# Packed weights unpacked in an earlier layer, biases spread out, two products and one load moved: a fused eight-layer kernel on one core

## What is computed

```python
# layer 1: attention, 16 heads of 96 (second_attention); then the rotated feed-forward
x = x + attention_1(norm(x), ctx)
x = x + (hadamard(norm(x)) @ W.T + b + lora(norm(x)))
# layer 2: attention, 32 heads of 128, queries and keys RMS-normed (wide_attention)
q, k = rmsnorm(norm(x) @ Wq.T), rmsnorm(ctx @ Wk.T)
x = x + softmax(q @ k.T / sqrt(128) + mask) @ v @ Wo.T
x = x + dequant(fp8(norm(x)) @ fp8(weight))         # quantised_ffn
# layer 3: autocorrelation attention (lag_attention); then a feed-forward on packed weights
x = x + lag_attention(norm(x), ctx)
w = interleave(words >> 4, words << 28 >> 28) * scale_of_each_64     # w1, w2, w3
x = x + (silu(norm(x) @ w1.T) * (norm(x) @ w3.T)) @ w2.T
```

## Time and profile before

| | us |
|---|---|
| median of 3 runs (1535.88 to 1538.91) | 1538.39 |
| the profiled execution, its own time | 1534.98 |
| the profiled execution, span of the instructions | 1533.3 |
| second_attention | 353.7 to 651.3 |
| rotated_ffn | 652.3 to 683.8 |
| wide_attention | 684.4 to 1206.1 |
| quantised_ffn | 1207.1 to 1247.5 |
| lag_attention | 1248.4 to 1352.9 |
| packed feed-forward | 1353.8 to 1533.3 |

### The profile page before, as it was taken

One profiled execution on the slowest core, in us unless ns is written; L12 is line 12 of the kernel. 1 busy time (PEld: TensorE's weight loads), 2 busy tenths in 40 slices (PEclk: granted clock), 3 DMA queues, 4 the chain that ended last, 5 costly groups with the idle time before them and its releaser, 6 DMA issues. The chain is left out here.

```text
span 1533.3 us, 31435 instructions
## 1 busy us (share of the span) xinstructions
PE 1386.9 (90%) x11352; PEld 829.4 (54%) x11352; DVE 1063.9 (69%) x2135; ACT 757.5 (49%) x2424; POOL 722.3 (47%) x750
## 2 busy tenths in 40 slices
PE   5888699997999999779999999999998777779998
PEld 4676344445777777335555555555554334334444
DVE  7997565635767666568878878788777779955212
ACT  4777363222424433338666666666654456555111
POOL 4887451002443444836666666666556115744000
PEclk9999699999999999989999999999999889989999
DMA  7999572215999988666667666555546302355000
GB/s 187 186 173 175 125 170 42 37 33 137 178 186 188 168 137 143 116 163 134 119 128 114 118 128 119 111 110 107 107 77 135 94 3 49 95 96 111 14 15 28
DMA packets 524137, 174.62 MB, mean 114 GB/s; under 512 B 482528, under 2 KB 507424, under 8 KB 523856
## 3 DMA queue, kind: packets, MB, share of 16 engines
q1 hardware_dynamic: 523984, 172.62, 58.4%
HBM read 53.27 MB, written 2.10 MB: 36 GB/s over the span
## 5 line engine op out<-in xcount | busy, mean ns | idle before, releaser
L1943 POOL TENSOR_TENSOR a_q_ss<-a_q_ss,half 128x4 f32<-128x4 f32 x64 | 90.1, 1408 | 170.0 <-DVE a_k_ss L1853 90.7
L67 PE MATMUL bank<-a_wq_hi,xn_pair 128*128 128x512 f16 (+1 forms) x384 | 139.8, 364 | 14.2 <-issue 8.3
L1767 ACT ACTIVATE a_probs<-a_masked,a_negmax 128x128 f32<-128x128 f32 x256 | 99.6, 390 | 96.9 <-DVE a_negmax L1824 96.9
L1286 POOL TENSOR_TENSOR a_p_hl<-a_probs,a_p_hl 128x512 f16<-128x512 f32 x64 | 74.3, 1161 | 142.4 <-DVE a_p_hl L1210 142.4
L69 PE MATMUL bank<-a_wq_hi,xn_pair 128*128 128x512 f16 (+1 forms) x384 | 139.6, 364 | 0.0
L68 PE MATMUL bank<-a_wq_lo,xn_pair 128*128 128x512 f16 (+1 forms) x384 | 139.6, 364 | 0.0
L67 PE MATMUL bank<-a_wo_hi,a_o_hi 128*128 128x512 f16 x256 | 98.4, 384 | 3.5 <-DVE x_state L1840 3.5
L68 PE MATMUL bank<-a_wo_lo,a_o_hi 128*128 128x512 f16 x256 | 98.0, 383 | 0.0
L69 PE MATMUL bank<-a_wo_hi,a_o_lo 128*128 128x512 f16 x256 | 97.9, 382 | 0.0
L1821 DVE TENSOR_TENSOR a_masked<-bank,a_mask 128x512 f32<-128x512 f32 x64 | 44.1, 690 | 70.5 <-PE bank L69 70.5
L1958 POOL TENSOR_TENSOR a_normal<-a_probs,a_recip 128x512 f32<-128x512 f32 x64 | 89.9, 1404 | 5.0
(11 more groups left out here) (465 smaller groups left out, 4993.9 us busy)
## 6 DMA issues: line engine op xcount, KB each, us to landing
a_no<-in_L_xattn_Wo SPq DMA_DIRECT2D x9, 1024.0 KB, 5.8
a_nq<-in_L_xattn_Wq SPq DMA_DIRECT2D x8, 1024.0 KB, 5.9
a_n_wq<-in_L_xattn_Wq SPq DMA_DIRECT2D x4, 768.0 KB, 6.1
a_n_wo<-in_L_xattn_Wo SPq DMA_DIRECT2D x4, 768.0 KB, 5.8
a_nk<-in_L_xattn_Wk SPq DMA_DIRECT2D x9, 256.0 KB, 3.0
a_nv<-in_L_xattn_Wv SPq DMA_DIRECT2D x9, 256.0 KB, 3.5
f_v_hat<-in_L_ffn_w SPq DMA_DIRECT2D x2, 1152.0 KB, 5.5
x_state<-in_x SPq DMA_DIRECT2D x8, 256.0 KB, 4.8
```

The source lines that it names most:

```text
L67: pe.matmul(out, lh, rh, start=start, stop=False)
L1286: pool.tensor_tensor(p_hl[s % PN][:, 1, t, :], probs[unit(s, t) % PROBS][:, :, :].rearrange("p h n -> p (h n)"), p_hl[s % PN][:, 0, t, :], ...
L1767: m = act.activation(probs[s % 2][:, h, :], src, ACT.Exp, bias=negmax[s % 2][:, h:h + 1], accum_out=total[s % 2][:, h:h + 1])
L1943: pool.tensor_tensor(r[:, :], r[:, :], K.half[:, 0:n], ALU.pow).then_inc(root_done.sem, 1)
```

## The change

1. **Biases.** The seven additions in `second_attention` become five, one row at each of the steps 30 to 34; rows 5 and 6 are added on POOL at the start of `rotated_ffn`, next to row 7.
2. **Turned rows.** The buffers of the normalised rows and their arrival semaphores go to `Rotated`. SP no longer waits at the end of `second_attention`; PE waits for each batch's row in `rotated_ffn`.
3. **Two query products.** `MADE` grows by the query products of the first two batches. They are made at the end of `rotated_ffn` on PE.
4. **Packed words.** A new class `PackedFirst` holds words, scales and the unpacking. SP loads them in wide attention (five transfers at step 0, then w2's words in four parts at steps 2, 4, 6 and 8). One of 13 pieces begins every 4 steps from step 3: DVE shifts at s and s + 2, ACT makes it 16-bit at s + 3, and for w1 and w3 POOL scales at s + 5, ACT splits at s + 6 and DVE at s + 7. All of this leaves `quantised_ffn` and `lag_attention`; what stays there is scaling and splitting of w2's chunks.
5. **First turns.** The two turns of w1 and w3 move from the end of `lag_attention`'s SP program to step 7.
6. **Context.** Its two loads move from step 62 to step 64, behind the turn of the probabilities of unit 63; the weight stays at 62.

```diff
@@ Rotated
+    XB, BIASED = 4, 5
@@ second_attention
-    BIAS_AT = {TOTAL + i: [2 * i - 2, 2 * i - 1] for i in range(1, 4)}
-    BIAS_AT[TOTAL + 4] = [6]
+    BIAS_AT = {ROWS_ROT + 2 + b: [b] for b in range(rot.BIASED)}
...
-                for b in range(rot.AHEAD - XB, rot.AHEAD):
-                    sp.wait_ge(next_in[b % XB], 16 * (b // XB + 1))
@@ wide_attention
+                    down.load(sp, s)
                     if s == LOAD:
...
                         quant.load_weight(sp, weight_in)
+                    if s == TOTAL:
                         quant.load_context(sp, quant_in)
...
+                    down.halves(act, s)
...
+                    down.unpack(dve, s)
...
+                    down.scale_first(pool, s)
@@ WideFirst
-    MADE = (("k", 0, 0), ("k", 0, 1))
+    MADE = (("k", 0, 0), ("k", 0, 1), ("q", 0), ("q", 1))
...
     def make(self, pe, use, bank):
+        if use[0] == "q":
+            b, H = use[1], self.A.heads
+            pe.wait_ge(self.lo_done.sem, self.lo_done.count(("wq", H - 1)))
+            pe.wait_ge(self.next_in[b], 16)
+            for k in range(KT):
+                m = pair_matmul(pe, bank[:, :], tuple(p[:, k, b * P:(b + 1) * P] for p in self.xn),
+                                tuple(p[:, k, 0:H * R] for p in self.w_p["wq"]), k == 0, k == KT - 1)
+            m.then_inc(self.made, 1)
+            return
@@ rotated_ffn
+                    else:
+                        pe.wait_ge(rot.next_in[b % rot.XB], 16 * (b // rot.XB + 1))
...
-                    if b == LAST:
-                        dve.wait_ge(last_biased, 1)
+                    if b in late:
+                        dve.wait_ge(biased.sem, biased.count(b))
...
+                for b in late:
+                    if b == LAST:
+                        pool.wait_ge(last_xn_done, 1)
+                    pool.tensor_tensor(K.x[:, b, :], K.x[:, b, :], rot.bias(), ALU.add).then_inc(biased.sem, 1)
@@ quantised_ffn
-                packed.load_down(sp, words_here)
-                packed.load_first(sp, words_here)
-                sp.wait_ge(words_here, 96)
@@ lag_attention
+                    if i == B - 1:
+                        sp.wait_ge(qb_bank.filled("x"), qb_bank.n_filled("x", B - 1))
+                        for m in ("w1", "w3"):
+                            packed.turn_first(sp, m)
...
-                for m in ("w1", "w3"):
-                    sp.wait_ge(down.lo_done.sem, down.lo_done.count(down.FIRST[m]))
-                    packed.turn_first(sp, m)
...
-                    for chunk in UNPACK.get(i, ()):
-                        down.to_half(act, chunk)
...
-                    for chunk in UNPACK.get(i, ()):
-                        down.unpack(dve, chunk)
...
-                        down.unpack(dve, W3)
...
-                down.scale(pool, W1)
-                down.scale(pool, W3)
-                down.low(pool, W1)
-                down.low(pool, W3)
@@ PackedFirst (new)
+    WORD_PARTS = [(0, 3), (3, 6), (6, 9), (9, 11)]
+    BEGIN = 3
...
+    def piece_at(self, s, late, every):
+        i, odd = divmod(s - self.BEGIN - late, every)
+        return [self.pieces[i]] if odd == 0 and 0 <= i < len(self.pieces) else []
...
+    def unpack(self, dve, s):
+        for part in range(2):
+            for n in self.piece_at(s, 2 * part, 4):
...
+                if part == 0:
...
+                    dve.tensor_scalar(dst[:, 0:g, 0, :], src, 4, None, ALU.arith_shift_right)
+                else:
+                    dve.tensor_scalar(dst[:, 0:g, 1, :], src, 28, 28, ALU.logical_shift_left,
+                                      ALU.arith_shift_right).then_inc(self.ints_done.sem, 1)
```

More of the change, by code:

```diff
@@ L2733, in _, with quantised_ffn @@
                         root(b)
-def quantised_ffn(K, Q, spectra, packed):
+def quantised_ffn(K, Q, spectra):
     nc, LAST = K.nc, B - 1
@@ L2752, in quantised_ffn @@
         row_mean, row_root, const_done = (K.sem(f"f2_{n}") for n in ("row_mean", "row_root", "const"))
-        largest_done, chain, words_here = (K.sem(f"f2_{n}") for n in ("largest", "chain", "words"))
+        largest_done, chain = (K.sem(f"f2_{n}") for n in ("largest", "chain"))
         one, along = sb("one", [1, 2], F32), sb("along", [1, 2, P], F32)
@@ L3222, in step @@
                         r.then_inc(row_mean_done, 1)
-                        down.unpack(dve, W1)
                     if l == B - 1:
@@ new lines, in __init__ @@
+        self.first = {n: m for m, n in self.FIRST.items()}
+        self.chunks = list(range(-(-self.HID * self.PER // self.CHUNK)))
+        self.pieces = list(self.first) + self.chunks
+        step = lambda n, of: Steps(K.sem(f"early_{n}"), of)
+        self.ints_done, self.half_done = step("ints", self.pieces), step("half", self.pieces)
+        self.scaled_done, self.hi_done, self.lo_done = (step(n, list(self.first)) for n in ("scaled", "hi", "lo"))
+        self.first_here, self.scales_here = K.sem("down_first_here"), K.sem("down_scales_here")
@@ new lines, in __init__, with groups, words_of, scales_of @@
+        self.words_here = [K.sem(f"down_words_here{i}") for i in range(len(self.WORD_PARTS))]
+    def groups(self, n):
+        return self.PER if n in self.first else min(self.PER, self.W2G - self.PER * n)
+    def words_of(self, n):
+        if n in self.first:
+            return self.first_words[self.first[n]][:, :]
+        at = self.CHUNK // 2 * n
+        return self.words[:, at:at + self.groups(n) * self.GROUP]
+    def scales_of(self, n):
+        at = 2 * self.PER * n
+        return self.scales[:, at:at + 2 * self.groups(n)]
@@ new lines, in halves @@
+    def halves(self, act, s):
+        for n in self.piece_at(s, 3, 4):
+            i = self.pieces.index(n)
+            act.wait_ge(self.ints_done.sem, self.ints_done.count(n))
+            act.activation(self.values(n), self.ints[i % 2][:, 0:self.groups(n), :, :].rearrange("p j h c -> p (j h c)"),
+                           ACT.Copy, scale=WS).then_inc(self.half_done.sem, 1)
+        for n in self.piece_at(s, 6, 4):
+            if n in self.first:
+                act.wait_ge(self.scaled_done.sem, self.scaled_done.count(n))
+                act.activation(self.first_halves[self.first[n]][:, 0, :], self.flat[self.pieces.index(n)],
+                               ACT.Copy).then_inc(self.hi_done.sem, 1)
@@ new lines, in scale_first @@
+    def scale_first(self, pool, s):
+        for n in self.piece_at(s, 5, 4):
+            if n in self.first:
+                by = self.first_scales[self.first[n]][:, :].unsqueeze(2).to_broadcast([P, 2 * self.PER, self.GROUP])
+                pool.wait_ge(self.half_done.sem, self.half_done.count(n))
+                pool.tensor_tensor(self.flat[self.pieces.index(n)].rearrange("p (j c) -> p j c", c=self.GROUP),
+                                   self.values(n).rearrange("p (j c) -> p j c", c=self.GROUP), by, ALU.mult).then_inc(self.scaled_done.sem, 1)
@@ L3408, in __init__ @@
         self.rows = rows[0:W.PER]
-        step = lambda n: Steps(K.sem(f"down_{n}"), self.pieces)
-        self.ints_done, self.half_done, self.scaled_done, self.hi_done, self.lo_done = (
-            step(n) for n in ("ints", "half", "scaled", "hi", "lo"))
+        step = lambda n: Steps(K.sem(f"down_{n}"), self.chunks)
+        self.scaled_done, self.hi_done, self.lo_done = (step(n) for n in ("scaled", "hi", "lo"))
         self.blank, self.turned = K.sem("down_blank"), W.turned
@@ L3837, in build @@
                 rotated_ffn(K, rot, nxt, first)
+                K.in_use.extend(rot.next_in)
                 K.end_stage()
-            stage_4_to_7(K, a, out, nxt, first, late)
+                K.in_use = kept
+            stage_4_to_7(K, a, out, nxt, first, late, down)
 def stage_0_to_1(K, a, early):
@@ L3853, in stage_2, with stage_4_to_7 @@
     K.in_use.extend(early.first_in.values())
-def stage_4_to_7(K, a, out, nxt, first, late):
+def stage_4_to_7(K, a, out, nxt, first, late, down):
     with ExitStack() as rows:
-        K.xn_rows = rows.enter_context(K.nc.sbuf_tensor("xn_rows", [P, B, DIM], F32))
         quant = Quantised(K, rows, a["L2_ffn_weight"], a["ctx_4096"])
-        wide_attention(K, W2, first, quant, nxt)
+        wide_attention(K, W2, first, quant, nxt, down)
         K.in_use.extend(first.sems())
```

152 lines of the change are left out of this document (67 added, 85 removed).

## The result

The changed kernel takes 1526.39 us (median of 4 runs, 1526.17 to 1527.74); the kernel before, timed beside it, 1538.65 (1535.88 to 1542.34). The ratio is 0.9923, with an interval of 0.9906 to 0.9939: 12.3 us less. The forecast was 1526.7 us, and 11.7 us less. Measured a second time, the changed kernel took 1525.6 against 1538.21, ratio 0.9913 (0.9899 to 0.9926), 12.6 us less.

The account below looks back on a forecast made before the run. PE bounds the middle of wide attention; at the joints, the stage's last engine or first awaited work does. Gains 2.0 - 0.8 + 0 + 3.0 + 3.7 + 3.8 = 11.7 us, from 1538.39 to 1526.7; range 1518 to 1533.

Parts of the forecast that it names:

- Biases and turned rows: End of second_attention: POOL's last additions no longer end the stage; gain 2.0 us, bounds 1.0 and 3.4.
- The delay carried through to the merge: second_attention: early additions delay the last probabilities' low half by 0.87 us; 1.4 us carried to PE's merge and DVE.
- Two query products: End of rotated_ffn grows by 0.8 us (0 to 1.5); wide attention's start gets nothing back, since PE waits there.
- The rival at 1521.5: Start of wide attention: PE was the bound, so 5.2 us of products count; 1521.5 us, chance 0.10.
- Packed words in wide attention: Middle of wide attention: loads and 26 shifts cost 0, hidden behind PE in DVE's 1.6 us idle per step.
- Context later: End of wide attention: unit 62's turn lands earlier, the mix starts 2.5 us earlier; gain 3.0 us, bounds 2.5 and 3.6.
- it escapes the half clock that followed PE's wait: End of wide attention: the mix's first matmul took 0.58 us against 0.38 at full clock; taken as 0.5 us gain.
- my 1190.44: End of wide attention: time when DVE's low half of unit 61 ends, frees the bank and lets the mix start.
- Start of the lag layer: Chunks before the first query product (2.1 us) and search (2.15) go; 3.7 us, between 3.2 and 4.2 by clock rise.
- End of the lag layer: Without the turns of weights SP ends with the rows; the end comes 3.8 us earlier (3.3 to 3.9).
- the two in which the gain is given back: Lag steps, last heads: half given back (1532.5 us, chance 0.09); nearly all given back (about 1537 us, chance 0.07).
- the slower one: Wide attention: shifts break PE's rhythm as DVE and POOL collide; 0.65 us each, 16.9 us, time 1543.6; chance 0.08.

Follow-up runs that it names:

- before: The kernel without this change, and its profiles (three were taken): median 1538.65 us beside the changed kernel; the first profiled execution took 1534.98 us.
- after: The changed kernel, mostly its first profile, against the kernel before: median 1526.39 us, ratio 0.9923; the profiled execution took 1526.54 us.

## Why the prediction was right, term by term

The forecast was 11.7 us in five terms. The stages of all profiles give 11.9 by their means (three profiles of before, and the seven to eleven changed ones that leave a stage's edit as it is), but not by the same terms.

| term | forecast | profile before to after | by means |
|---|---|---|---|
| end of second_attention | -2.0 | -1.0 | -2.0 |
| rotated_ffn | +0.8 | -1.1 | +0.3 |
| wide attention, start and middle | 0 | 0 | 0 |
| wide attention, end | -3.0 | -2.4 | -1.2 |
| quantised_ffn | 0 | +0.7 | -0.2 |
| lag layer | -7.5 | -7.6 | -8.6 |
| packed ffn | 0 | +0.5 | -0.2 |

- **Biases and turned rows: right in size by the means; most of the carried delay in after has a cause that I didn't name.** POOL no longer ends the stage; PE's merge and DVE's low halves do, as the forecast has it. The delay carried through to the merge is 2.5 us in after, not 1.4, so that this pair of profiles gives the lower bound of 1.0. It is made of two things: the mix behind the last probabilities comes 0.78 us later, for the addition in front of their low half, and the output product behind it takes 3.8 us where it took 2.1, since PE falls to half clock there. The first is the step that I reckoned at 0.87. The second differs between executions, and I had no term for it. Undoing the part cost 4.1 us in its one run, of which POOL's end behind SP's last turn is 2.4. SP's removed wait has no run of its own.
- **Two query products: right.** The end of `rotated_ffn` moved from SP to PE by 0.84 us in after; compared at like clock the stage pays 0.5 (31.41 against 30.93, 33.07 against 32.58), where I had 0.8. The -1.1 of the first pair of profiles is clock: before runs its first products there at half clock in all three profiles (mean 0.66 over the first 8 us in the first), after at full clock in its first (1.00). Wide attention gets nothing back: PE reaches full occupation at the same 34.15 us behind the barrier's release, and only waits longer before that. The rival at 1521.5 falls with it.
- **Packed words in wide attention: right.** PE shows no gap between 731 and 1162 us, and making the shifts twice changes nothing. The shifts were slower than most in the lag layer, 0.70 and 1.13 us by the medians, and DVE's busy time grew by 24.1 us, on an engine that idled 88. The Trainium skill's page "GPSIMD Engine Reference", section "Key points", says that GpSimd shares its SBUF interfaces with VectorE, with contention for DVE instructions in a 2-port mode or with two SBUF inputs; the trace agrees, since the 26 shifts take 25.2 us where I had worked out 24 for all of them being slow.
- **Context later: mis-sized.** The step that failed is "it escapes the half clock that followed PE's wait" together with the 2.60 us of that wait: both were read from one profile, and its wide attention, at 522.3, was the longest of the three. In the other two the turn landed about 1 us earlier in the stage; PE waited 1.56 and 1.48 us for it and kept full clock behind the wait. The order of events is as forecast (the mix waits for DVE next, and the context lands in time), but DVE lets the mix begin 507.4 us into the stage in after, where my 1190.44 is 506.7. Against the two later profiles the gain is 0.7 and 0.4 us, and 1.2 by the mean of three, below the lower bound of 2.5.
- **Start of the lag layer: a little more than forecast.** The first query product comes 2.4 us earlier in the stage (I had 2.1, and left out the chunks of step -2), and the first search 4.8 in after. The last batch's transposes of weights come 3.8 us earlier in after, and 4.8 by the means of three and ten profiles, where I had 3.7 between 3.2 and 4.2. I had taken the middle between two cases, a clock that rises when it did before and one that rises earlier with the work; the windows above show the second, 2.7 us earlier in after. By the granted clock 2.4 GHz is back 16.8 to 17.9 us into the stage in the three profiles of before, 13.1 to 14.6 in eight changed ones and 16.3 in two. The Trainium skill's page "TensorE: Matmul & The Clock Gate", Part 1, says that activity releases the throttle, by which the rise would come earlier along with the work; the traces agree in eight of these ten, and the two others have the longest layers (98.2). The chunks of steps 0 and 1 were put back in no run.
- **End of the lag layer: right to the tenth.** 8.81 - 5.01 = 3.80 us, against 3.8.

So the time met the forecast closely because errors cancelled: the context was taken 1.8 us too high by the means, the lag layer 1.1 too low, the rotated layer 0.5 too high a loss. Of the rivals, the two in which the gain is given back fall with the lag layer's 8.6 us, and the slower one with PE's full window, which held with each shift made twice. What stays open is how the 4.1 us of the late biases divide beyond the 2.4 of POOL's end: the kernel was profiled once.

## What to carry to other kernels

Move work out of the joints between stages, where one engine works and the others wait, into a stretch that another engine fills without a gap; there even slow operations cost nothing in this kernel, with DVE busy for 85 to 88% of the stretch. Making products ahead was worth nothing here, since the stage that they were taken from begins with a chain of other engines. Before a term of two or three us is read from one profile, look whether it holds a stretch at half clock, and take a second profile.

## What was unexpected on the hardware

TensorE's clock falls to 1.2 GHz at places that can differ between executions of the same program. For `second_attention` (298.3 or 300.5 us in the kernel before) and `rotated_ffn` (31.4 or 33.1 in the changed one, with the same wait in front) the windows above show it; of the lag layer's 96.9 to 98.2, the two longest are the two in which the clock came back last, 16.3 us into the stage. Also, PE's wait for the same turned probabilities behind the same 3 MB, which I had taken for fixed, was 2.60, 1.56 and 1.48 us in three executions and ended 509.2, 508.3 and 508.0 us into the stage.
